# A Mamba-2 and expert kernel on one core: reordered joints between its stages, and the scan's state held as two blocks on 128 partitions

## The reference

```python
def _mamba2(u, ...):                       # u: layernorm of h
    zxbcdt = u @ in_w.T
    z, xBC, dt = jnp.split(zxbcdt, [D_INNER, D_INNER + CONV_DIM], axis=-1)
    dt = jax.nn.softplus(dt + dt_bias)
    xBC = _silu(causal_conv4(xBC) + conv_b)
    xh, Bm, Cm = jnp.split(xBC, [D_INNER, D_INNER + D_STATE], axis=-1)
    dA = jnp.exp(dt * A)
    def step(state, inputs):               # 8 heads x 64 x 64
        state = dA_t[:, :, None, None] * state + (dt_t[:, :, None] * x_t)[..., None] * B_t[:, None, None, :]
        y_t = jnp.einsum('bhpn,bn->bhp', state, C_t)
        return (state, y_t)
    ...
    y = (y + Dp * xh) * _silu(z)
    return rms(y) * rms_w @ out_w.T
```

## Time and profile before

| | us |
|---|---|
| median of 3 runs (lowest, highest) | 1446.47 (1441.79, 1446.49) |
| the profiled execution's own time | 1445.83 |
| its span in the trace | 1443.9 |
| PE busy | 1300.4 (90% of the span) |
| DVE busy | 1098.9 (76%) |
| ACT busy | 797.2 (55%) |
| POOL busy | 801.1 (55%) |
| chain that ended last: PE / DVE / issue / POOL | 54% / 21% / 10% / 7% |

### The profile page before, as it was taken

How to read it: one execution, slowest core, us unless ns; L and a number is a source line. 1 busy time by engine, 2 the same in 40 slices (tenths; PEclk the granted TensorE clock), 3 DMA queues, 4 the chain that set the end, 5 groups by cost and what they waited for, 6 DMA issues and landing times.

```text
span 1443.9 us, 39948 instructions
## 1 busy us (share of the span) xinstructions
PE 1300.4 (90%) x13112; PEld 1033.6 (72%) x13113; DVE 1098.9 (76%) x2564; ACT 797.2 (55%) x1821; POOL 801.1 (55%) x738
## 2 busy tenths in 40 slices
PE   3889999999999999999988799999999999999980
PEld 1456556566666666666667789999999999999970
DVE  4879999999999999899967686666566656565537
ACT  4666665665756766577635344445444544444435
POOL 3457677667676878687774342425062506153771
PEclk9999999999999999999967999999999999999985
DMA  6303432334443243312234331303113212202594
GB/s 176 112 30 118 131 102 86 106 107 126 132 132 118 66 126 116 121 63 99 89 132 170 98 109 40 116 30 98 54 46 100 95 55 76 73 29 66 139 205 149
DMA packets 94656, 145.73 MB, mean 101 GB/s; under 512 B 13488, under 2 KB 77488, under 8 KB 94448
## 3 DMA queue, kind: packets, MB, share of 16 engines
q1 hardware_dynamic: 79216, 97.06, 21.2%
q0 software_dynamic: 15072, 46.51, 11.0%
q10 hardware_dynamic: 288, 1.19, 0.2%
HBM read 103.06 MB, written 41.67 MB: 100 GB/s over the span
## 4 chain that ended last, share of the span: by engine, by line
PE 54%; DVE 21%; issue 10%; POOL 7%; ACT 3%; DMA 1%; SPq 1%; DVEq 1%; POOLq 0%; ACTq 0%
PE pe L1076 12%; PE pa L1076 12%; PE py L1101 11%; DVE arena L1637 3%; PE pa L659 3%; POOL arena L2552 3%; DVE arena L1676 3%; PE pa L651 3%; PE py L794 2%; PE pm L830 2%; PE pt L812 2%; PE pz L781 1%; DVE arena L1703 1%; DMA arena<-queue 1%; DVE arena L1684 1%
## 5 line engine op out<-in xcount | busy, mean ns | idle before, releaser
L1076 PE MATMUL pe<-arena 128*128 128x128 f16 x3408 | 222.1, 222 | 18.2 <-issue 17.2
L1076 PEld LDWEIGHTS pe<-arena 128*128 128x128 f16 x3408 | 206.1, 99 | 23.5 <-issue 21.7
L1076 PE MATMUL pa<-arena 128*128 128x128 f16 x3408 | 219.7, 220 | 2.2 <-issue 2.0
L1520 ACT ACTIVATE arena<-pe,arena 128x128 f32<-128x128 f32 x568 | 162.0, 371 | 76.9 <-PE pe L1076 75.3
L1076 PEld LDWEIGHTS pa<-arena 128*128 128x128 f16 x3408 | 202.2, 98 | 2.5 <-issue 2.1
L1101 PE MATMUL py<-arena 128*128 (+1 forms) x1704 | 197.5, 273 | 1.2 <-DVE arena L2289 1.2
L1637 DVE SCALAR_TENSOR_TENSOR arena<-pa,arena 128x511 f32<-128x511 f32 (+2 forms) x240 | 178.5, 745 | 8.2 <-ACT arena L1172 2.1
L1101 PEld LDWEIGHTS py<-arena 128*128 128x128 f16 x1704 | 163.5, 98 | 19.3 <-issue 1.7
L2252 DVE SCALAR_TENSOR_TENSOR pm<-pa,arena 128x128 f32<-128x128 f32 x284 | 80.4, 351 | 98.0 <-ACT arena L1520 83.2
L1676 DVE TENSOR_TENSOR_SCAN arena<-arena,pe 128x512 f32<-128x512 f32 x128 | 148.7, 1202 | 3.3 <-issue 1.9
L2452 POOL TENSOR_SCALAR arena<-arena 128x1536 f16<-128x1536 f32 (+2 forms) x35 | 42.7, 1219 | 190.9 <-DVE arena L2289 178.9
(11 more groups left out here) (297 smaller groups left out, 2548.8 us busy)
## 6 DMA issues: line engine op xcount, KB each, us to landing
arena<-step_rows SPq DMA_DIRECT2D x64, 512.0 KB, 6.4
arena<-in_w_exp POOLq DMA_DIRECT2D x32, 768.0 KB, 4.7
arena<-queue SPq DMA_DIRECT2D x74, 129.5 KB
answer<-arena SPq DMA_DIRECT2D x71, 128.0 KB, 1.7
arena<-in_x SPq DMA_DIRECT2D x16, 512.0 KB, 6.6
answer<-zeros SPq DMA_DIRECT2D x10, 512.0 KB, 4.8
arena<-h SPq DMA_DIRECT2D x9, 512.0 KB, 6.1
h<-arena SPq DMA_DIRECT2D x8, 512.0 KB, 3.0
```

What stands on the lines that cost most here:

```text
L1076: ins = pe.matmul(bank[:, f * P:(f + 1) * P], w_split[:, p, hl, d * 2 * FF + col:d * 2 * FF + col + P], x[:, r, d, :], start=(n == 0), sto ...
L1520: ins = e.activation(sg[:, half, f, :], GATE[half][:, f * P:(f + 1) * P], ACT.Silu, bias=b1a[:, bass.ds(ex_, 1), ff], scale=1.0 / S1)
```

## The change

**The state.** `state`, its scaled copy and `cT` take all 128 partitions. Heads 0 to 3 stand in rows 0 to 63 with columns 0 to 255, heads 4 to 7 in rows 64 to 127 with columns 256 to 511, and the rest is zero. `chunk_s` becomes two products of 256 columns, to partitions 0 to 63 and 64 to 127 of `pz`; `first_state` and `next_state` become two instructions each; `conv_silu` of c4 writes `cT` a second time; `chunk_z` contracts over 128 rows.

**The start.** The norm parameters come in two small transfers and GpSimd spreads them (`widen`). ScalarE waits for the other parameters only after both `ln_out`. The input weights are split in halves by k. GpSimd does `scale_out`, and `high_out(0)`, `low_out(0)` and the statistics of sequence 1 come later.

**The last unit and the epilogue.** VectorE takes `chunk_b1` and `g_low` ahead of `scan(2)`, and the statistics after `chunk_b1(2)`. GpSimd takes `x_d(1)`, `add_xd(1)` ahead of `old_state(1)` and `first_weights`, and the scatters later. SyncE loads `b2` after the lead's rows and waits for `g_ready`. `turn(0, 0)`, `rows_out` and `rows_low` come earlier.

**The plan.** The sum over experts is one scan; each step stands one or more places earlier, and the row numbers are given out on their own (`rows_done`) ahead of the rest.

```diff
@@ SyncE
-            for dst, src in ((lnw, ln_w), (lnb, ln_b)):
-                param(dst[:, 0:NB], src[:, 0:1].to_broadcast([P, NB, KD]))
-                param(dst[:, NB:2 * NB + 1], src[:, 1:2].to_broadcast([P, NB + 1, KD]))
+            for n, src in enumerate((ln_w, ln_b)):
+                sp.dma_start(ln_two[:, n], src).then_inc(ln_in, 16)
...
-                    sp.wait_ge(ss_ready, NK * MAMBA_UNITS)
+                    sp.wait_ge(g_ready, NK * MAMBA_UNITS)
                     sp.dma_start(b1a, b1).then_inc(bias_in, 16)
-                    sp.dma_start(b2a, b2.unsqueeze(0).to_broadcast([P, NE, D])).then_inc(bias_in, 16)
...
                         lead_rows(first, j)
+                    sp.dma_start(b2a, b2.unsqueeze(0).to_broadcast([P, NE, D])).then_inc(bias_in, 16)
...
-            sp.wait_ge(plan_done, 1)
+            sp.wait_ge(rows_done, 1)
@@ TensorE
-                pe.matmul(pz[:, :], cT[0:DS, c.q, c.k * P:(c.k + 1) * P],
-                          state[0:DS, (c.k - 1) % 2].rearrange("p h d -> p (h d)"),
+                pe.matmul(pz[:, :], cT[:, c.q, c.k * P:(c.k + 1) * P],
+                          state[:, (c.k - 1) % 2].rearrange("p h d -> p (h d)"),
...
-                pe.matmul(pz[0:DS, :], bs[:, q, k, :], xw[:, kq].rearrange("p h d -> p (h d)"),
-                          start=True, stop=True).then_inc(z_full, 1)
+                for rows_, heads in HALVES:
+                    ins = pe.matmul(pz[rows_, heads.start * HD:heads.stop * HD], bs[:, q, k, :],
+                                    xw[:, kq, heads].rearrange("p h d -> p (h d)"), start=True, stop=True)
+                ins.then_inc(z_full, 1)
...
-                do_fills(st, ["lg"])
...
                 chunk_z(c[3])
+                do_fills(st, ["lg"])
...
-                chunk_d(Chunk(st.before, NK - 1))
+                c3 = Chunk(st.before, NK - 1)
+                pe.wait_ge(pt_free, c3.use("o") + 1)
                 turn(0, 0)
+                chunk_d(c3)
@@ ScalarE
-                    ins = e.activation(cT[0:DS, vq], acc[DS:P, mq], ACT.Silu)
+                    e.activation(cT[0:DS, vq], acc[DS:P, mq], ACT.Silu)
+                    ins = e.activation(cT[DS:P, vq], acc[DS:P, mq], ACT.Silu)
...
-                e.activation(state[0:DS, 0].rearrange("p h d -> p (h d)"), pz[0:DS, :], ACT.Copy).then_inc(z_free, 1)
+                for rows_, heads in HALVES:
+                    ins = e.activation(state[rows_, 0, heads].rearrange("p h d -> p (h d)"),
+                                       pz[rows_, heads.start * HD:heads.stop * HD], ACT.Copy)
+                ins.then_inc(z_free, 1)
...
-                high_out(0)
+                rates()
                 softplus(st)
...
                 z_silu(st, 0)
+                high_out(0)
                 ln_apply(1, 1)
...
-            e.wait_ge(params, 16 * N_PARAMS)
-            e.activation(aneg, aneg, ACT.Exp).then_inc(c_prep, 1)
             e.wait_ge(win_in[0], 16 * KD)
-            high_in(0)
+            for k in range(KD):
+                high_in(0, k)
@@ VectorE
-                dve.tensor_tensor(state[0:DS, kq], pz[0:DS].rearrange("p (h d) -> p h d", h=NH), state_d[0:DS],
-                                  ALU.add).then_inc(z_free, 1)
+                for rows_, heads in HALVES:
+                    ins = dve.tensor_tensor(state[rows_, kq, heads], pz[rows_].rearrange("p (h d) -> p h d", h=NH)[:, heads],
+                                            state_d[rows_, heads], ALU.add)
+                ins.then_inc(z_free, 1)
...
                 choose_lead()
                 end_add(st)
-                scan(c[2])
                 chunk_b1(c[1])
                 g_low(c[0])
+                scan(c[2])
                 chunk_mix(c[2])
-                ch3 = s3_stats(st)
                 chunk_b2(c[1])
                 next_state(c[1])
                 chunk_b1(c[2])
+                ch3 = s3_stats(st)
                 scan(c[3])
...
-                dve.tensor_copy(plan_f[0:1, 3 * NJT + NE:3 * NJT + 2 * NE], end[0:1, :])
                 step(dve.tensor_tensor(row_f, tmpj[0:1], jd, ALU.add))
+                dve.tensor_copy(plan_i[0:1, 0:NJT], row_f).then_inc(rows_done, 1)
@@ GpSimd
                 x_dt(c[1])
+                x_d(c[1])
+                add_xd(c[1])
                 old_state(c[1])
                 first_weights()
-                scatter_before(st, 0, 1)
-                scatter_before(st, 1, 3)
-                x_d(c[1])
-                add_xd(c[1])
-                rsqrt_x1(st)
-                scatter_before(st, 3, 4)
                 x_dt(c[2])
                 gated(c[1])
...
+            pool.memset(state.rearrange("p a h d -> p (a h d)"), 0.0)
...
+            def widen():
+                pool.wait_ge(ln_in, 32)
+                for n, dst in enumerate((lnw, lnb)):
+                    for l, first, end_ in ((0, 0, NB), (1, NB, 2 * NB + 1)):
+                        ins = pool.tensor_copy(dst[:, first:end_], ln_two[:, n, l:l + 1].to_broadcast([P, end_ - first, KD]))
+                ins.then_inc(ln_wide, 1)
```

More of the change, by code:

```diff
@@ L399, in build @@
         hop = sem("hop")
-        plan_done = sem("plan_done")
+        rows_done, plan_done = sem("rows_done"), sem("plan_done")
         padded = sem("padded")
@@ L1158, in ln_out @@
                 w, wq = (st.u + 2, st.q) if ahead else (0, 0)
+                if not ahead and d == 0:
+                    e.wait_ge(ln_wide, 1)
                 e.sem_inc(hop, 1)
@@ L1862, in prologue @@
             def prologue(st):
-                ln_stats(1, 0, 1)
                 dt_first(st)
+                dve.wait_ge(c_prep, 1)
+                dve.tensor_scalar(aneg, aneg, -1.0, None, ALU.mult).then_inc(c_prep, 1)
+                dve.wait_ge(c_prep, 2)
                 ch1 = Chain(dve, c_dve2, S1_LINKS, st.u + 1)
                 dt_last(st, ch1)
-                low_out(0, prepared)
                 taps(st, "c4", ch1)
@@ L1875, in prologue @@
                 scan(Chunk(st, NK))
+                low_out(0, prepared)
                 chunk_mix(Chunk(st, NK))
@@ L2028, in epilogue @@
                 low_parts(2)
+                low_parts(3)
+                rows_low(0, 0)
+                weigh_rows(0, 0, lead[:, 0:1])
                 roots(3, NK, 2)
@@ L2033, in epilogue @@
                 root_rows(st)
-                low_parts(3)
-                rows_low(0, 0)
-                weigh_rows(0, 0, lead[:, 0:1])
                 s3_top(st, ch3)
@@ L2137, in ends_of_places @@
             def ends_of_places():
-                step(dve.tensor_copy(end[:, 0:1], nt_p[:, 0:1]))
-                for e in range(1, NE):
-                    step(dve.tensor_tensor(end[:, e:e + 1], end[:, e - 1:e], nt_p[:, e:e + 1], ALU.add))
+                step(dve.tensor_tensor_scan(end, ones[:, 0:NE], nt_p, 0.0, ALU.mult, ALU.add))
             def places():
@@ L2192, in plan_out @@
                                        AX.X, ALU.add))
-                dve.tensor_copy(plan_i[0:1, :], plan_f[0:1, :]).then_inc(plan_done, 1)
+                step(dve.tensor_copy(plan_f[0:1, 3 * NJT + NE:3 * NJT + 2 * NE], end[0:1, :]))
+                dve.tensor_copy(plan_i[0:1, NJT:], plan_f[0:1, NJT:]).then_inc(plan_done, 1)
             def rows_moved():
@@ L2557, in prologue @@
                 u_low(0, 0, st, "ln1")
+                scale_out()
                 rsqrt_ln(1)
@@ L2701, in epilogue, with scale_out @@
                 scatter(NB - 1, 1, 0, 2 * NK)
+            def widen():
[4 more added lines that the diff above has]
+                ins.then_inc(ln_wide, 1)
+            def scale_out():
+                pool.wait_ge(params, 16 * N_PARAMS)
+                next_(pool.tensor_scalar(rmsw, rmsw, S2 / SG, 0.0, ALU.mult, ALU.add))
+                pool.wait_ge(wout_in, 32)
+                for l in range(2):
+                    for c in range(NCT):
+                        ins = pool.tensor_scalar(wout_raw[l][:, c, :], wout_raw[l][:, c, :], rmsw[:, l, c:c + 1], 0.0,
+                                                 ALU.mult, ALU.add)
+                    ins.then_inc(wout_scaled, 1)
+            widen()
             rsqrt_ln(0)
```

79 lines of the change are left out of this document (41 added, 38 removed).

## The result

The changed kernel takes **1435.91 us** (median of 6 runs, 1433.71 to 1441.14) beside 1446.03 us for the kernel before (6 runs, 1441.79 to 1449.14): ratio 0.9943, 95% interval 0.9923 to 0.9963. It is faster by 0.6%, 8 to 10 us, where 19 were forecast. A second measurement of the same kernel gave 1438.26 us and a ratio of 0.9940 (0.9918 to 0.9962). The profiled execution took 1441.14 us, the slowest of its six, with a span of 1439.5; so the two spans stand only 4.4 us apart, and I read the places one by one.

A forecast was written before the change was run, and what follows sets the result against it. Bound changes by stage: PE alone in the expert tiles, PE and VectorE nearly full in the units, the rest in joints. 1445.8 - 3 (start) - 8 (last unit) - 8 (plan) + 0 (body) = 1427 us; range 1410 to 1438.

The forecast's parts named there:

- The start, -3: Head of unit 0: parameters stop delaying ScalarE, dt_first comes 7.3 us earlier, about 3 put back; -3 us, ends -5 and -1.5.
- The last unit, -8: Last unit and epilogue: three terms, sum 8.3 us, taken as -8; far end -12, near end -4.
- The first term, -4.2: Last unit: PE's 4.21 us wait at chunk_z(2) for next_state(1) goes, as add_xd(1) moves ahead of loads and scatters.
- The second and third, -3.2 and -0.9: Epilogue: lead's rows, no longer behind b2, arrive faster, -3.2 us; gate_bank's 0.99 us wait for rows_low shrinks, -0.9 us.
- a sign of being wrong: Prediction wrong if the last unit is bound by the scatters, or the units' stretch moves by more than 10 us.
- the joints' gain stays behind: Rival, chance 0.12: scatters end as late, last unit gives 0 to 4 us, start is eaten; 1437 us.
- The plan, -8: Before tile (2, 0): PE's 6.18 us wait goes, two banks gain 1 us each from the clock; sum 8.2 us.
- I allow up to 3 us: Plan: allowance for GpSimd's second-expert split starting some 5 us earlier and disturbing VectorE; sets the near end, -5.
- The body, 0: Units: chunk_s saving and added VectorE time alike, 0.2 us a unit each way; 0, between -10 and +10.
- side by side in full: Rival, chance 0.17: chunk_s halves overlap wholly and PE is what the units wait for; -12, 1415 us.
- the serial case: Units: chunk_s halves run one behind the other, same streaming plus one change of weights, up to 0.15 us.
- VectorE's term: Units: next_state as two instructions costs at most +0.18 us, twice a unit, with one of a unit on the chain.

The follow-up runs named there:

- old joints: Kernel before (1446.03 us) and kernels changing only its state part, such as the change's state alone (1447.04 us) or the half-column state with full-height chunk_z (1431.19 us).
- joints, early split: Changed kernel, GpSimd splitting the second expert's weights after rows_done: 1435.91 and 1438.26 us; the same with the state put back as before: 1433.65 us, ratio 0.9929.
- joints, late split: Changed kernel with GpSimd waiting for plan_done, not rows_done, before splitting the second expert's weights: 1430.73 us, ratio 0.9887; also versions of it with other states.
- the single 128x256 addition and no wait: State in half the columns, chunk_z as two full-height products: 1422.22 us with changed start, last unit, plan and split after plan_done; 1431.19 us on the kernel before.
- The joints with the late split and the old state: Changed kernel with the second expert's split after the whole plan and the state as in the kernel before: 1427.27 us, ratio 0.9891; again 1428.23 us, ratio 0.9884.

## Why the prediction was half right

The forecast was -19 us and -8 to -10 came. Three parts of the span in us, lowest to highest over all profiles with the same joints, whatever their state:

| | old joints (7 profiles) | joints, early split (3) | joints, late split (7) |
|---|---|---|---|
| start to unit 1 | 55.9 to 58.1 | 54.9 to 59.5 | 55.0 to 57.9 |
| unit 15 to the gate | 94.4 to 98.8 | 90.2 to 96.3 | 90.7 to 96.4 |
| gate to the end | 670.2 to 674.0 | 669.7 to 671.1 | 662.9 to 666.8 |

Units 1 to 15 go by the state: 611.7 to 615.1 us with the old one, 616.5 to 620.2 with the change's, 603.3 and 603.4 with the single 128x256 addition and no wait.

- **The start, -3: mechanism right, size too large.** `dt` came at 19.88 for 19.5, and `steps` of unit 0 began 4.1 us earlier (25.61 for 29.70). But unit 0 itself took 29.5 to 33.9 us in all profiles with the new start and 27.0 to 28.4 without it, so that in the mean unit 1 began 1 us earlier: some 3 of the 4.1 us went back. The two profiles of the change have 1.4 later (the head of its unit 0 at a clock of 0.50) and 1.0 earlier. The term's own working was loose too: 3 of 7.3 us put back leave 4.3, not 3.
- **The last unit, -8.** The first term, -4.2, came (4.21 to 0.55 us; 36.0 to 32 us at like clock). The second and third, -3.2 and -0.9, are a step that failed: from `chunk_y(3)` to the gate it takes 22.3 and 23.7 us in the two profiles of the change where it took 23.4. "The lead's rows are issued behind the 1 MB of `b2`" was right: they are quicker by 2.6 to 2.8 us. But they are not asked for earlier. The eighth scatter is issued behind `gated(3)` as before (755.74 for 755.26), and SyncE, freed of its wait for ScalarE, now waits 4.8 us for the scatters. And PE had used the transfer's time: `chunk_d` ran ahead of the turn and now runs behind it, so the gate starts 6.6 and 7.9 us after the turn instead of 5.1. That the last unit is bound by the scatters was a sign of being wrong that the prediction had named, and it is the rival "the joints' gain stays behind", for this half of the term. Both are read from the timelines; no run puts the scatters or the turn elsewhere. Of the 8.1 us that the first profile shows, 4 are the wait and 4 the clock.
- **The plan, -8: the step that failed most.** "I allow up to 3 us" for GpSimd's earlier split was the mis-sized term. It takes all but 1.5 to 2.9 us of the gain. The split started some 9 us earlier, counted from the first gate, not 5. The plan's last steps are a chain of small VectorE instructions, and four rows of one or two of them take as long as GpSimd's instruction beside them (1.48, 1.55, 3.17 and 2.73 us, against 0.15, 0.38, 0.38 and 0.21 ahead of the late split), so `plan_done` came 3.9 us after PE asked for it (823.85 for 819.91), not 3 us before. With the split behind the plan the term came to 5.8 to 9.7 us, 7.5 in the mean, beside the 8 of the sum.
- **The body, 0: the state costs 3 us by itself** (units 1 to 15, 617.88 for 614.92), and the change has +5.2 and +1.8. The halves of `chunk_s` do run side by side and save 0.41 us each, as in the rival *side by side in full*; neither the serial case nor its 0.15 us came (1.01 us on the same rows, for 1.00). The 0.15 was my estimate of one more change of weights; the weight loads of `chunk_s` last 134 ns in the mean from 102 to 480 before, and no run shows one added to the time. Yet the period grew. The failed step is VectorE's term: 0.18 us with one `next_state` of a unit on the chain was forecast, 0.28 us each with both on it was measured (0.60 to 0.88), 0.56 us a unit. PE's saving of 1.2 us a unit gave some 0.2 back, which leaves the 0.34. The third silu costs nothing, as said; `chunk_z` over 128 rows takes 622 ns a record where it took 639.

The two profiles of the change are 4.4 and 4.0 us shorter than the one before; the rest of the measured -8 to -10 is that both were the longest executions of their six. The joints with the late split and the old state, in which the plan keeps its cover and the state costs nothing, give 1427.27 and 1428.23 us, beside the forecast of 1427. That is in part luck: of their two profiles the start has -2.8 and -2.3, the last unit -7.5 and -5.8 (with the clock's share in it), the plan -6.6 and -7.2, and units 1 to 15 add -3.2 and -2.0 that nobody forecast.

## What to carry to other kernels

When a wait is loosened, ask first what the freed work now runs beside: here two links of a chain, 0.38 us by themselves, took 3.17 us beside one GpSimd instruction of 3.11. When a transfer is made shorter, look at what the engine that waited did in the meantime and at what the request itself waits for. Where two engines are both over 90% busy, as here, a saving on one can be worth a sixth of itself (0.2 of 1.2 us); taking one instruction off tells which to relieve. When a layout makes an operation two instructions, look for the layout in which it is one: the same idea lost 0.34 us a unit with two additions and won 0.75 with one.

## What the runs showed of the hardware

- Two fp32 products of 256 columns to rows 0 to 63 and 64 to 127 of one PSUM bank take 0.59 us to their successor, to the same 64 rows 1.01. They overlap in the main; half of 1.01 would be the whole overlap.
- A pair of 64x256 VectorE additions out of PSUM takes 0.88 us to its successor with the second on rows 64 to 127, and 0.66 us with both on rows 0 to 63; the instructions around the pair start at row 0. One 128x256 addition takes 0.33 us, one of 64x512 0.60. The added 0.22 us comes with the other rows; no run shows why, and I had not weighed it.
- VectorE instructions of 24 to 72 elements on one partition (L2181, L2183, L2185 and L2200; one or two to a row) take 1.48 to 3.17 us a row, until the GpSimd instruction beside them ends, and 0.15 to 0.38 us where no GpSimd instruction runs.
- One `chunk_z` split in two 64-row products, with a wait between its halves, which write one bank, lost 0.46 us each (12.4 us in 27). The same without the wait was not tried.
